# Splitting two batches' folded attention weights in layer 1's attention stage instead of in layer 0's blocks

## What is computed

```
x = x + tanh(g_xattn[0]) * auto_correlation_attention(layernorm(x), ctx)
x = x + tanh(g_ffn[0])   * moe0(layernorm(x))     # 8 experts, top 2, and a shared expert
x = x + tanh(g_xattn[1]) * attention(layernorm(x), ctx, mask)   # 16 heads of 64
x = x + tanh(g_ffn[1])   * moe1(layernorm(x))     # 32 experts, top 4, 256 slots each, and a shared one
```

## Time and profile before

| | us |
|---|---|
| median of 3 runs | 1052.3 (1049.78 to 1059.98) |
| profiled execution, first to last instruction | 1055.6 |
| PE busy | 895.3 (85%) |
| DVE busy | 648.2 (61%) |
| GpSimd (POOL) busy | 551.9 (52%) |
| ACT busy | 495.7 (47%) |

### The profile page before, as it was taken

How to read it: one execution, slowest core, us unless ns; L and a number is a source line. 1 busy time by engine, 2 the same in 40 slices (tenths; PEclk the granted TensorE clock), 3 DMA queues, 4 the chain that set the end, 5 groups by cost and what they waited for, 6 DMA issues and landing times. The chain is left out here.

```text
span 1055.6 us, 18563 instructions
## 1 busy us (share of the span) xinstructions
PE 895.3 (85%) x5465; PEld 753.2 (71%) x5465; DVE 648.2 (61%) x2128; ACT 495.7 (47%) x1781; POOL 551.9 (52%) x634
## 2 busy tenths in 40 slices
PE   4998768999998598888459899999999978999940
PEld 3563447888887488787358799999999966888720
DVE  4603034787787555464258889999999963444441
ACT  1313663444442244454257667877887741222200
POOL 1400122576677135455546866666666653877861
PEclk8978988999999798899779999999999979999985
DMA  9621875589889667986298944514426204899688
GB/s 307 201 94 51 247 209 142 129 250 253 267 237 272 209 209 220 252 300 216 96 227 206 247 122 170 177 65 152 117 66 197 85 14 115 156 222 246 80 201 162
DMA packets 157812, 189.70 MB, mean 180 GB/s; under 512 B 16035, under 2 KB 137017, under 8 KB 157714
## 3 DMA queue, kind: packets, MB, share of 16 engines
q1 hardware_dynamic: 109810, 121.87, 39.9%
q0 software_dynamic: 30720, 46.46, 20.5%
q10 hardware_dynamic: 17184, 20.19, 5.7%
HBM read 96.19 MB, written 103.63 MB: 189 GB/s over the span
## 5 line engine op out<-in xcount | busy, mean ns | idle before, releaser
L1875 POOL DMA_INDIRECT slots_d<-rows,place x128 | 133.4, 1042 | 65.7 <-DVE place L2095 34.5
L1934 ACT ACTIVATE att<-bank,mx 128x77 f32<-128x77 f32 x512 | 160.9, 360 | 1.2 <-DVE mx L2011 1.1
L997 POOL DMA_INDIRECT y_d<-rows x78 | 77.6, 995 | 96.3 <-DVE rows L1375 71.5
L1934 ACT ACTIVATION_READ_ACCUMULATOR att<-bank,mx 128x1 f32 x512 | 123.6, 241 | 0.0
L957 POOL DMA_INDIRECT slots_d<-rows,place x64 | 63.9, 998 | 19.0 <-issue 18.8
L1397 PE MATMUL bank<-wd_hi,act_hi 128*128 128x256 f32 (+1 forms) x206 | 68.5, 332 | 2.7 <-DVE act_lo L1370 1.4
L1889 POOL DMA_INDIRECT acc_d<-expert_out,target_rows x32 | 49.6, 1551 | 26.2 <-issue 25.4
L1399 PE MATMUL bank<-wd_hi,act_lo 128*128 128x256 f32 (+1 forms) x206 | 60.1, 292 | 0.0
L1398 PE MATMUL bank<-wd_lo,act_hi 128*128 128x256 f32 (+1 forms) x206 | 60.0, 291 | 0.0
L2011 DVE TENSOR_REDUCE mx<-bank 128x6 f32<-128x462 f32 (+1 forms) x96 | 55.3, 576 | 5.6 <-PE bank L2195 5.2
L1889 POOL DMA_INDIRECT result<-expert_out,target_rows x32 | 49.5, 1547 | 16.9 <-DMA result<-expert_out,target_rows 8.1
(11 more groups left out here) (322 smaller groups left out, 2998.2 us busy)
## 6 DMA issues: line engine op xcount, KB each, us to landing
rows<-slots_d SPq DMA_DIRECT2D x39, 260.0 KB
slots_d<-zrow SPq DMA_DIRECT2D x8, 1168.0 KB
expert_rows<-slots_d SPq DMA_DIRECT2D x32, 292.0 KB
expert_gate_up<-in_wgu SPq DMA_DIRECT2D x28, 256.0 KB
x_res<-y_d POOLq DMA_DIRECT2D x14, 512.0 KB
wqk_d<-wqk SPq DMA_DIRECT2D x32, 154.0 KB
vwo_d<-vwo SPq DMA_DIRECT2D x16, 308.0 KB
x_res<-in_x SPq DMA_DIRECT2D x8, 512.0 KB
```

Of the source, the lines that this page charges most:

```text
L997: pool.indirect_dma_start(y0_d, bass.IndirectOffsetOnAxis(ap=x_rows(s)[:, b, D:D + 1].bitcast(I32), axis=0), y_rows(s, b), None, bounds_ch ...
L1875: pool.indirect_dma_start(slots_d, bass.IndirectOffsetOnAxis(ap=place[:, n % 3, k:k + 1], axis=0), rows[:, n % 3, :], None, bounds_check=S ...
L1934: last = act.activation(att[:, par, h * S:(h + 1) * S], bank[:, a, i * S:(i + 1) * S], ACT.Exp, scale=-1.0, bias=mx[:, par, h:h + 1], accu ...
```

## The change

The last twelve pieces, batches 2 and 3, leave stage two; only batches 0 and 1 are split there. In the attention SP loads the plain matrices of batches 2 and 3 into the low half of their buffers (`load_folded`, at tiles 8 and 16). Seven pieces a batch (`fold_piece`: three of the scores of 822 columns or one less, three of the values with 768, one rest of 80 rows and 256 columns), one a step from step 10 to 16 and from 18 to 24, are split there: ACT copies the low half's range into the high half, rounded, at the head of the step (`split_folded`), and GpSimd subtracts it from the low half in place, between `rstd_b` and the dispatches. PE waits for GpSimd's count (`fold_lo`) where it waited for the loads.

```diff
-PIECES = 6 * B
+PIECES = 12
...
-            DENSE_PARTS = 2 * (CHUNKS - 1)
-
-            def block_part(s, phase):
-
-                q = DENSE_PARTS + s // 4
-                return q if s % 4 == phase and q < PIECES else None
...
-                        if 2 * c < DENSE_PARTS:
+                        if 2 * c < PIECES:
...
-                    part_high(2 * c - 2)
                     gated(c, 2)
...
-                    part_high(2 * c - 1)
-                    store_part(2 * c - 2)
-                    store_part(2 * c - 1)
...
-                        if block_part(s, 1) is not None:
-                            part_high(block_part(s, 1))
-                        if block_part(s, 3) is not None:
-                            store_part(block_part(s, 3))
...
-                        if block_part(s, 2) is not None:
-                            part_low(block_part(s, 2))
...
+            fold_hi, FHI = uv_mm, B + PIECES
+            fold_lo, FLO = uv_out, 2 + PIECES
+            fold_in, FIN = part_in, [PIN + 16 * dmas(PIECES - 2), PIN + 16 * dmas(PIECES - 1)]
+            FOLD_PIECES = 7
+
+            def fold_piece(n):
+
+                b, i = n // 8 + 1, n % 8 - 2
+                if i < 0:
+                    b, i = b - 1, i + 8
+                if not B // 2 <= b < B or i >= FOLD_PIECES:
+                    return None
+                j = i % 3
+                if i < 3:
+                    buf, cols, p1 = (scores0, scores1)[b % 2], (0, 822, 1643, KD * HS), P
+                    at, half = slice(cols[j], cols[j + 1]), KD * HS
+                else:
+                    buf, half = (values0, values1)[b % 2], JC * D
+                    p1 = P if i < 6 else JL
+                    at = slice(3 * j * D, 3 * (j + 1) * D) if i < 6 else slice((JC - 1) * D, JC * D)
+                low = slice(half + at.start, half + at.stop)
+                return b, i, FOLD_PIECES * (b - B // 2) + i, buf[0:p1, at], buf[0:p1, low]
...
+                    def load_folded(b):
+                        want(sp, e_mm, 3 * 8 * (b - 1))
+                        sp.dma_start((scores0, scores1)[b % 2][:, KD * HS:].bitcast(F32).rearrange("p (k n) -> p k n", k=KD),
+                                     wqk_d[b].rearrange("(k p) n -> p k n", p=P)).then_inc(fold_in[0], 16)
+                        want(sp, av_mm, 8 * (b - 1))
+                        w = vwo_part(b, 1)
+                        sp.dma_start(w[:, 0:(JC - 1) * D].bitcast(F32).rearrange("p (j n) -> p j n", n=D),
+                                     vwo_d[b, 0:(JC - 1) * P, :].rearrange("(j p) n -> p j n", p=P)).then_inc(fold_in[1], 16)
+                        sp.dma_start(w[0:JL, (JC - 1) * D:].bitcast(F32), vwo_d[b, (JC - 1) * P:HS, :]).then_inc(fold_in[1], 16)
...
-                        if n % 8 == 2 and b < B:
-                            want(sp, e_mm, 3 * 8 * (b - 1))
-                            load_scores(sp, b, (scores0, scores1)[b % 2])
-                        if n % 8 == 4 and b < B:
-                            want(sp, av_mm, 8 * (b - 1))
-                            load_values(b)
+                        if n == 2:
+                            load_scores(sp, 1, scores1)
+                        if n == 4:
+                            load_values(1)
+                        if n % 8 == 0 and B // 2 <= b < B:
+                            load_folded(b)
...
+                        if fold_piece(n) is not None:
+                            b, i, q, high, low = fold_piece(n)
+                            pool.wait_ge(fold_hi, FHI + q + 1)
+                            pool.tensor_tensor(low, low.bitcast(F32), high.bitcast(F32), ALU.subtract).then_inc(fold_lo, 1)
...
+                    def split_folded(n):
+                        b, i, q, high, low = fold_piece(n)
+                        if i < 3:
+                            act.wait_ge(fold_in[0], FIN[0] + 16 * (b - 1))
+                        else:
+                            act.wait_ge(fold_in[1], FIN[1] + 32 * (b - 1))
+                        act.activation(high, low.bitcast(F32), ACT.Copy).then_inc(fold_hi, 1)
+
                     def step(n, par, scores, values, routes, dispatch):
+                        if fold_piece(n) is not None:
+                            split_folded(n)
```

More of the change, by code:

```diff
@@ L148, in build @@
         vwo_d = nc.dram_tensor("vwo_d", (B, HS, D), F32, kind="Internal").ap()
-        wqk_hi_d, wqk_lo_d = (nc.dram_tensor(f"wqk_{part}_d", (B, D, HS), F32, kind="Internal").ap() for part in ("hi", "lo"))
-        vwo_hi_d, vwo_lo_d = (nc.dram_tensor(f"vwo_{part}_d", (B, HS, D), F32, kind="Internal").ap() for part in ("hi", "lo"))
+        wqk_hi_d, wqk_lo_d = (nc.dram_tensor(f"wqk_{part}_d", (B // 2, D, HS), F32, kind="Internal").ap() for part in ("hi", "lo"))
+        vwo_hi_d, vwo_lo_d = (nc.dram_tensor(f"vwo_{part}_d", (B // 2, HS, D), F32, kind="Internal").ap() for part in ("hi", "lo"))
         slots_d = nc.dram_tensor("slots_d", (CAP + SLOTS, ROW), F32, kind="Internal").ap()
@@ L899, in _ @@
                     sp.wait_ge(cleared, 16 * (2 * (CHUNKS - 1) + 1 + E0))
[L900 to L904, removed]
+                    for s in range(BLOCKS):
                         if s >= NX:
@@ L1346, in _ @@
                     product(c, 2)
-                    part_low(2 * c - 2)
                     low_part(c, 2)
@@ L1351, in _ @@
                     low_part(c, 3)
-                    part_low(2 * c - 1)
                     add_shared(c)
@@ L2210, in score @@
                         if a == 0:
-                            pe.wait_ge(wqk_in, 32 * (n // 8 + 1))
+                            b = n // 8
+                            if b < B // 2:
+                                pe.wait_ge(wqk_in, 32 * (b + 1))
+                            else:
+                                pe.wait_ge(fold_lo, FLO + FOLD_PIECES * (b - B // 2) + 3)
                             pe.wait_ge(a_xT, n + 1)
@@ L2236, in values_mm @@
                     def values_mm(n, par):
-                        pe.wait_ge(vwo_in, 64 * (n // 8 + 1))
+                        b = n // 8
+                        if b < B // 2:
+                            pe.wait_ge(vwo_in, 64 * (b + 1))
+                        else:
+                            pe.wait_ge(fold_lo, FLO + FOLD_PIECES * (b - B // 2 + 1))
                         want(pe, av_added, n)
```

## The result

The kernel after takes 1060.66 us (median of 4 runs, 1060.33 to 1061.03), the kernel before 1053.25 us in the same comparison (4 runs, 1049.78 to 1059.98): ratio 1.0085, 95% interval 1.0051 to 1.0119. The forecast was 1061 us. The profiled execution of after took 1061.03 us and spans 1059.3; before's profile spans 1055.6 us. A span is 1.7 to 2.1 us shorter than the execution's time in the runs listed, so before's profiled execution was one of some 1057.5 us, 4 us over its median, and after's was at its median.

What follows compares the result with a forecast made beforehand. It took GpSimd's scattering plus its gaps to bound layer 0's blocks and DVE the attention; on the profiled execution 1055.6 - 13 + 22 = 1064.6 us, its +9 carried to the 1052.3 median as 1061 us, range 1040 to 1079.

Steps and rivals of the forecast that it cites:

- The sum: Whole kernel: -13 us from layer 0 and +22 us in the attention, +9 us in all, giving 1061 us.
- Attention, +22: Layer 1's attention: GpSimd's subtraction stalls DVE for its whole length in 14 steps, +22 us, bounds +2 and +31.
- the first of the two orders that were named: Attention step: GpSimd's subtraction gets in first and DVE's row normalisation L2045 is held for 1.8 us.
- No hold, the rival of 1041: Attention: DVE is not held by GpSimd's subtraction, -13 + 2, 1041 us; chance 0.13.
- The lower bound of +2: Attention without a hold: dispatches start 1.1 us later against 0.96 us of slack, 0.15 us a step, +2 us.
- ACT's copy, nothing: Attention step's head: the 0.88 us copy fits in ACT's 1.62 us wait for shift_a, costing nothing.
- The loads: Attention: plain-weight loads of batches 2 and 3 land in time, the new wait covered by 3 us.
- Blocks, -10: Layer 0's gathered blocks: 13 gaps for 16 (8 us) and two long gaps 1 us shorter each, 10 us gained.
- Entry, -3: Entry to layer 0's blocks: first rows land sooner without stores of pieces 12 and 13, 3 us gained (0 to 5).
- Rival 1: Layer 0's blocks are paced by the scatters, so only the entry gains: -3 + 22, 1071 us; chance 0.20.
- rival 3: Layer 0's blocks give nearly all of their bound through less traffic: -27 + 22, 1047 us; chance 0.17.
- the upper bound: Attention: DVE's hold lasts 0.6 us longer than GpSimd's recorded time, 2.4 us in twelve steps, +31 us.

Runs made afterwards that it cites:

- e2: Kernel before plus only the attention's part of the change, layer 0 left alone; ratio to before 1.0168, +17.7 us.
- e1: Kernel after with GpSimd's subtraction moved behind its wait for the place column, ahead of the four dispatches; ratio to before 1.0002.
- e12: Kernel after without GpSimd subtraction: ACT writes the negative rounded piece, DMAs add the plain matrix, rstd_a and shift_a between dispatches; ratio to before 1.0101.
- e9: Kernel before without pieces 12 and 13, ten pieces kept in the blocks, attention reading batches 0 and 1 twice; ratio to before 0.9968.
- e8: Kernel before without the ten pieces of the blocks, pieces 12 and 13 kept, attention reading batches 0 and 1 twice; ratio to before 0.9977.
- e3: Kernel before with only layer 0's part of the change, pieces 12 to 23 out, attention reading batches 0 and 1 twice; ratio 0.9914, -9.1 us.
- e7: Kernel before with only GpSimd's rstd_a and shift_a of the next tile moved between the second and third dispatch; ratio to before 0.9944.

## Why the prediction was right

**The sum.** Forecast 1061, measured 1060.7; +9 us over before, measured +0.85% (9.0 us). The spans of the two profiles differ by only 3.7 us, since before's lay over its median and after's did not. The total came out nearer than its terms, and that is luck: the attention was put 3 to 4 us too high and layer 0's gain 4 us too high.

- **Attention, +22: right in mechanism, high by 3.** The trace shows the first of the two orders that were named: L2045 (now L2070) is held, and not the cast behind it. The piece took longer than said (1.95 and 1.82 us for 1.8 and 1.7), but the step grew by only 1.61 and 1.49, since an instruction of 0.41 us would have run in that time anyway: it ends with the subtraction instead of after it. I had added the whole subtraction. Measured 19.4 from the steps, 18.9 over the stage, 17.7 in time (e2). Steps of 11.2, not 11.5.
- **No hold, the rival of 1041:** excluded by the rows of `norm_b`. Its 0.15 us a step looks too low as well: in e1, where nothing is held and the dispatches start 1.4 us later (the bound had 1.1), the steps grew by 0.7 to 0.9 us, because `shift_a` stands behind the dispatches. The lower bound of +2 left that chain out.
- **ACT's copy, nothing: right, as far as the rows show.** 1.22 to 1.28 us of idle time are left behind it in the wide steps, and 0.62 and 0.86 in the first of each batch. In e12 even two passes a step were covered, at another place.
- **The loads: covered, right.** No wait of ACT or GpSimd for them is in the list of waits.
- **Blocks, -10: the two profiles agreed (133.8 us for 143.1), the reason did not.** I expected 13 gaps for 16, and two long ones shorter by 1 us each. There are 15 gaps over 1 us for 16, and they are shorter, 2.6 us for 2.9: shorter rather than fewer. (My 15 gaps of 2.7 us for DVE's rows had one of 0.30 us among them that is none.) Split by releaser, the 9.3 us are 3.6 from waits for DVE's rows, 2.1 from waits of GpSimd's issue, 1.7 from the scatters themselves (973 ns for 995) and 1.9 from a wait for ACT's rows that is gone. And the size was luck of two profiles: over nine, the scatters' stretch is 4 us shorter, in ranges that overlap. This is the term that was mis-sized most.
- **Entry, -3: -5.0 in the two profiles, -4.8 over the nine.** The size is within the 0 to 5 given. The cause that I gave, the stores of pieces 12 and 13 ahead of the first rows, isn't borne out: without them (e9) the distance was 29.2 us, with them and no block pieces (e8) 30.8, and only with all twelve gone 22.8 to 28.1. Entry and blocks together are -8.7 in the profiles and -9.1 in time (e3), where I had -13.
- **Rival 1, only the entry gains (1071),** failed on e3's time; **rival 3, -27 in layer 0 (1047),** failed by a factor of three. The waits of ACT for something unnamed stayed (22.7 us in six pieces between 380 and 515 us, 23.6 in seven before), and their cause stays unknown.

So two errors, +3 to +4 in the attention and -4 in layer 0, cancel almost wholly. What stays open is which resource of layer 0 the pieces compete for: removing the engines' work, the bytes or the stores, each alone, changed nothing that could be measured, nor did either group of pieces much.

## What to carry to other kernels

Before giving GpSimd streaming work, list what DVE does at that very time: beside instructions that read PSUM it was free for DVE, beside a scalar form from SBUF to SBUF it cost nearly its own length (1.61 us for 1.94), and moving one wait changed which. Then follow what stands behind it on GpSimd, since the next limit was a small `shift_a` at the end of its queue. A bursty stage isn't to be judged by one profile: six of the same code spread over 9.7 us, and only the timed halves settled what it gave.

## What the runs showed of the hardware

- DVE's scalar form from SBUF to SBUF, started just behind GpSimd's subtraction, is held for the whole of it, one to one with width (411 columns: 1.16 us, 821: 2.02 us, alone: 0.41). DVE's hold ends 0.15 us after GpSimd's recorded end, not the 0.6 us of the upper bound.
- It goes the other way too: a one-column GpSimd instruction took 1.56 us in place of 0.57 when DVE's 924-column multiply with two SBUF inputs started at the same time. When GpSimd was 0.07 us ahead, it took 0.57, and the multiply kept its 1.12 us. The Trainium skill ("SBUF — State Buffer", section "Who interferes with whom") has the block as mutual, the first to issue as the winner and the other fully blocked. The held instructions here agree with that; the multiply, second at 671.18 and not blocked, does not.
- GpSimd's dispatches (indirect DMAs) take part in it: in e7 one that starts 0.14 us behind DVE's multiply takes 1.93 us for 0.97, and in before DVE's 32-column `mselb` takes 0.34 us for 0.18 and ends with the dispatch beside it.
- GpSimd streams 821 columns in 1.92 us and 411 in 1.07, so some 2.1 ns a column and 0.2 us fixed.
- An adding DMA of 384 KB, DRAM to SBUF, issued from GpSimd at 700.28 had landed by 706.66, 6.4 us later.
